# A linear-attention and expert block: x2 goes over DRAM to be turned on VectorE, with new orders on all engines

## What is computed

```python
h = layernorm(x) * (1 + ca) + sa
q, k = elu(h @ Wq.T + bq) + 1, elu(h @ Wk.T + bk) + 1;  v = h @ Wv.T + bv      # 16 heads of 32
KV = sum_s k v ;  Z = 1 / (q . sum_s k + 1e-6)
x1 = x + ga * ((q KV Z) @ Wo.T + bo)
x2 = layernorm(x1)
V  = (x2 * (1 + cb) + sb) @ fWv.T + fbv                                         # 512 wide
r, c = V @ Wg.T + bg, norms of 8 probes of 8 of V                               # 8 experts
w  = softmax over the top 2 of  ln(r) + sigmoid(alpha) * ln(c)
out = x1 + gb * (V + sum_e w_e * (silu(V @ W1_e.T + b1_e) @ W2_e.T + b2_e))
```

## Time and profile before

| what | value |
|---|---|
| median of three runs | 1216.82 us |
| the profiled execution: its time, its span | 1216.84 us, 1215.1 us |
| TensorE, VectorE busy over the span | 1202.4 us (99%), 1001.0 us (82%) |
| GpSimd, ScalarE busy over the span | 609.1 us (50%), 545.0 us (45%) |
| DMA queues | 34.6% of 16 engines, 108 GB/s |
| granted TensorE clock | 9 or more tenths in all 40 slices |

### The profile page before, as it was taken

How to read it: one execution, slowest core, us unless ns; L and a number is a source line. 1 busy time by engine, 2 the same in 40 slices (tenths; PEclk the granted TensorE clock), 3 DMA queues, 4 the chain that set the end, 5 groups by cost and what they waited for, 6 DMA issues and landing times.

```text
span 1215.1 us, 18365 instructions
## 1 busy us (share of the span) xinstructions
PE 1202.4 (99%) x5680; PEld 987.7 (81%) x5680; DVE 1001.0 (82%) x2218; ACT 545.0 (45%) x1127; POOL 609.1 (50%) x458
## 2 busy tenths in 40 slices
PE   8999999999999999999999999999999999999998
PEld 5888878787877787887778888888888888888887
DVE  6988788988889888886788888888887888888775
ACT  4455454454454545454534343443434343443432
POOL 1443433333333443444556575766657576675741
PEclk9999999999999999999999999999999999999999
DMA  6565544444343343443231322313232231322201
GB/s 225 166 192 180 159 129 143 139 138 125 111 131 107 119 129 120 124 139 112 79 96 61 96 77 81 104 53 104 63 95 88 70 105 53 105 70 88 87 19 53
DMA packets 128515, 131.65 MB, mean 108 GB/s; under 512 B 12233, under 2 KB 82289, under 8 KB 128417
## 3 DMA queue, kind: packets, MB, share of 16 engines
q1 hardware_dynamic: 128416, 130.47, 34.6%
HBM read 80.62 MB, written 49.81 MB: 107 GB/s over the span
## 4 chain that ended last, share of the span: by engine, by line
PE 85%; DVE 5%; issue 4%; ACT 3%; DMA 1%; POOL 1%; SPq 0%; POOLq 0%; DVEq 0%; ACTq 0%
PE ps L1637 26%; PE ps L1638 26%; PE ps L1644 26%; PE ps L1853 3%; PE ps L1845 1%; DMA wm_in<-in_L_wmod_dram 1%; PE ps L1745 1%; DVE zk L1306 1%; DMA q_in<-q_scratch 1%; ACT exp_k L859 1%; ACT exp_q L830 1%; DVE qf L1282 1%; ACT exp_q L832 1%; POOL cn L725 1%; ACT exp_k L861 0%
## 5 line engine op out<-in xcount | busy, mean ns | idle before, releaser
L696 POOL TENSOR_TENSOR xn_lo<-xn,xn_hi 128x512 fp32r<-128x512 f32 x64 | 85.9, 1342 | 279.6 <-ACT xn_hi L821 279.6
L725 POOL TENSOR_TENSOR cn<-c,half 128x16 f32<-128x16 f32 x32 | 104.1, 3254 | 189.8 <-DVE c L1405 189.8
L830 ACT ACTIVATE exp_q<-qf 128x512 f32<-128x512 f32 x64 | 40.5, 632 | 150.5 <-DVE qf L1282 150.3
L1637 PE MATMUL ps<-wk_hi,xT_hi 128*128 128x512 f32 x256 | 101.8, 398 | 2.3 <-ACT xT_hi L815 2.3
L1637 PE MATMUL ps<-g_hi,qT_hi 128*128 128x512 f32 x256 | 103.2, 403 | 0.1
L1637 PE MATMUL ps<-v_hi,xT_hi 128*128 128x512 f32 x256 | 103.0, 402 | 0.0
L1637 PE MATMUL ps<-k_hi,xn_hi 128*128 128x512 f32 x256 | 102.7, 401 | 0.0
L1637 PE MATMUL ps<-wq_hi,xT_hi 128*128 128x512 f32 x256 | 102.5, 400 | 0.1
L1638 PE MATMUL ps<-wq_lo,xT_hi 128*128 128x512 f32 x256 | 101.4, 396 | 0.0
L1638 PE MATMUL ps<-wk_lo,xT_hi 128*128 128x512 f32 x256 | 101.3, 396 | 0.0
L1638 PE MATMUL ps<-k_lo,xn_hi 128*128 128x512 f32 x256 | 100.6, 393 | 0.0
(11 more groups left out here) (250 smaller groups left out, 3333.8 us busy)
## 6 DMA issues: line engine op xcount, KB each, us to landing
xin<-_attn_hidden_states_dram SPq DMA_DIRECT2D x64, 256.0 KB, 3.1
q_scratch<-qf SPq DMA_DIRECT2D x64, 256.0 KB, 3.3
xin<-_attn_hidden_states_dram SPq DMA_DIRECT2D x32, 512.0 KB, 4.2
q_in<-q_scratch SPq DMA_DIRECT2D x128, 128.0 KB, 2.9
out_dram<-qf SPq DMA_DIRECT2D x64, 256.0 KB, 2.0
xn_scratch<-xn SPq DMA_DIRECT2D x62, 256.0 KB, 2.0
xq<-xn_scratch SPq DMA_DIRECT2D x248, 64.0 KB, 2.5
wm_in<-in_L_wmod_dram SPq DMA_DIRECT2D x4, 1024.0 KB, 6.1
```

The source lines that it names most:

```text
L696: nc.gpsimd.tensor_tensor(moved(xn_lo[:, 1 - s, :], i + 1), kept(xn[:, 1 - s, :], i + 1), moved(f32(xn_hi[:, 1 - s, :]), i + 1), ALU.subtr ...
L725: nc.gpsimd.tensor_tensor(cn[:].rearrange("p h e -> p (h e)"), c2[:].rearrange("p h e -> p (h e)"), half[:], ALU.pow).then_inc(cn_done, 1)
L830: nc.scalar.activation(exp_q[:, s, :], zq[:, s, :], ACT.Relu, scale=-1.0).then_inc(rq_done, 1)
L1637: nc.tensor.matmul(dst, ah, bh, start=start and n == 0, stop=False)
```

## The change

For the pairs 3 to 30, x2 isn't turned by TensorE any more. ScalarE writes the normalised tile in another order of its 32-column blocks, SyncE stores it to a scratch in DRAM (`x2_store`), loads it back in four pieces with the blocks regrouped over the partitions (`x2_load`, into the new buffer `x2q`), and VectorE turns the 32x32 blocks into the PSUM bank (`turned_x2`), where ScalarE and VectorE split it as before. The two `turn_hidden` of a pair become one, with five transposes in a row, and the high and low parts of both halves are taken by one instruction each (`aT_high(j)`, `aT_low(j)`, 512 wide). `qT_low` moves to GpSimd for the first pairs too. The orders of all five engines are new: on TensorE both `out_product` come first in a step and `fused_product` behind them; on VectorE `scores` and `weights` of a pair stand together at the end of the step; on GpSimd the power of the probes stands behind `queries_low`, and `q_times_ks` of pair j + 3 follows directly on `biased_x` of pair j + 1.

Left out of the diff are declarations, the waits that go with the new counts and the code ahead of the first full step. The functions `step_b` of GpSimd, ScalarE, VectorE and TensorE stand with their new text alone, in this order; the old ones stand above.

```diff
+            sp.wait_ge(qz_done, 3)
+            q_load(4)
+            sp.wait_ge(xb_done, 3)
+            bx_load(3)
+            def x2_store(j, h):
+                sp.wait_ge(x2_done, 2 * j + h + 1)
+                sp.dma_start(x2_dram[rows(2 * j + h), :], xn[:, h, :]).then_inc(x2_out[h], 16)
+            def x2_load(j, h):
+                sp.wait_ge(x2_out[h], 16 * (j - 2))
+                wait_count(sp, x2T_turned, 2 * (j - 4) + h + 1)
+                for i in range(KB):
+                    sp.dma_start(x2q[DH * i:DH * (i + 1), h, :].rearrange("p (g f) -> p g f", f=P),
+                                 x2_dram[rows(2 * j + h), i * P:(i + 1) * P].rearrange("(g t) f -> t g f", t=DH)).then_inc(x2_back[h], 16)
+            def result_store(j, h):
+                sp.wait_ge(fin_done, 2 * j + h + 1)
+                sp.dma_start(ot[rows(2 * j + h), :], out_t[:, h, :]).then_inc(stored[h], 16)
-                if live(j + 2, J):
-                    sp.wait_ge(qz_done, j + 1)
-                    q_load(j + 2)
-                if live(j + 1, J):
+                if live(j + 3, J):
+                    sp.wait_ge(qz_done, j + 2)
+                    q_load(j + 3)
+                if j > 2 and live(j + 1, J):
-                for h in range(2):
-                    if live(j - 2, J):
-                        sp.wait_ge(fin_done, 2 * (j - 2) + h + 1)
-                        sp.dma_start(ot[rows((j - 2) * 2 + h), :], out_t[:, h, :]).then_inc(stored[h], 16)
+                if live(j, J) and not by_pe(j):
+                    for h in range(2):
+                        x2_store(j, h)
+                        x2_load(j, h)
+                        result_store(j - 2, h)
+                else:
+                    for h in range(2):
+                        if live(j - 2, J):
+                            result_store(j - 2, h)
...
+            queries_low(3)
             def step_b(j):
                 if live(j + 2, J):
                     q_times_ks(j + 2)
+                if live(j + 1, J):
+                    queries_low(j + 1)
                 if live(j, J):
                     row_scale(j)
+                probe_norms(j - 1)
+                router_scale(j - 1)
                 if live(j + 1, J):
                     biased_x(j + 1)
+            sweep_pairs(step_b, 3, J)
...
-                act.wait_ge(x2T_psum, t + 1)
+                if j < FIRST_TURNED:
+                    act.wait_ge(x2T_psum, t + 1)
+                elif by_pe(j):
+                    act.wait_ge(x2T_psum, 2 * FIRST_TURNED + h + 1)
+                else:
+                    act.wait_ge(x2T_turned, 2 * (j - FIRST_TURNED) + h + 1)
...
+            def aT_high(j):
+                act.wait_ge(aT_psum, j + 1)
+                wait_count(act, y_psum, 2 * j)
+                nc.scalar.copy(wT_hi[:], bank_qaT[:, 2 * P:3 * P])
+                nc.scalar.copy(aT_hi[:], two_aT).then_inc(aTh_done, 1)
...
-                wait_count(act, x2T_psum, t - 1)
+                if j <= FIRST_TURNED:
+                    wait_count(act, x2T_psum, t - 1)
+                else:
+                    act.wait_ge(x2_out[h], 16 * (j - FIRST_TURNED))
...
-                nc.scalar.activation(xn[:, h, :], x1_of(j, h), ACT.Identity, bias=shift[:, h:h + 1],
+                dst, src = (xn[:, h, :], x1_of(j, h)) if by_pe(j) else (quarters(xn[:, h, :]), natural(x1_of(j, h)))
+                nc.scalar.activation(dst, src, ACT.Identity, bias=shift[:, h:h + 1],
...
             def step_b(j):
+                if j > 3 and live(j + 1, J):
+                    qT_high(j + 1, 0)
                 if live(j, J):
                     deviations(j, 0)
+                if j > 3:
+                    x2T_high(j - 1, 1)
+                if j == 3:
+                    qT_high(4, 0)
+                if live(j + 1, J):
+                    qT_high(j + 1, 1)
                 if live(j, J):
                     deviations(j, 1)
                     variances_eps(j)
+                aT_high(j - 2)
+                if live(j + 2, J):
+                    den_plus_eps(j + 2)
+                functions(j - 1)
+                if live(j, J):
                     normalised(j, 0)
                     normalised(j, 1)
                 if live(j, J):
                     x2T_high(j, 0)
+                exponentials(j - 1)
+            sweep_pairs(step_b, 3, J)
+            aT_high(J - 1)
         @block.vector
...
+            def turned_x2(j, h):
+                dve.wait_ge(x2_back[h], 64 * (j - 2))
+                dve.wait_ge(x2Tl_done, 2 * j + h)
+                dve.wait_ge(aTl_done, j - 1)
+                nc.vector.transpose(bank_x2T.rearrange("p (j g t) -> p g j t", j=KB, g=KB),
+                                    x2q[:, h, :].rearrange("p (g j f) -> p g j f", g=KB, j=KB)).then_inc(x2T_turned, 1)
...
+            def aT_low(j):
+                dve.wait_ge(aTh_done, j + 1)
+                nc.vector.tensor_tensor(aT_lo[:], two_aT, f32(aT_hi[:]), ALU.subtract).then_inc(aTl_done, 1)
...
             def step_b(j):
                 if live(j, J):
                     residual(j, 0)
+                if j == 3:
+                    scaled_q(4)
+                    turned_q(4)
+                elif not by_pe(j - 1):
+                    turned_x2(j - 1, 1)
                 if live(j, J):
                     residual(j, 1)
+                if j > 3:
+                    x2T_low(j - 1, 1)
                 if live(j + 2, J):
                     denominators(j + 2)
+                biased(j - 1, 0)
+                aT_low(j - 2)
+                if live(j + 2, J):
+                    inverses(j + 2)
+                biased(j - 1, 1)
+                probes(j - 1)
+                gated(j - 1)
+                finished(j - 2, 0)
+                if live(j + 2, J):
+                    scaled_q(j + 2)
+                finished(j - 2, 1)
+                variances(j - 1)
+                if live(j + 2, J):
+                    turned_q(j + 2)
+                if live(j, J) and not by_pe(j):
+                    turned_x2(j, 0)
                 if live(j, J):
                     x2T_low(j, 0)
+                scores(j - 1)
+                weights(j - 1)
+            sweep_pairs(step_b, 3, J)
+            aT_low(J - 1)
             finished(J - 1, 0)
             finished(J - 1, 1)
...
-            def turn_hidden(j, h):
-                t = 2 * j + h
+            def turn_hidden(j):
-                if bank_h(j, h) is bank_qaT:
-                    wait_count(pe, aTl_done, t)
-                else:
-                    pe.wait_ge(x2Tl_done, t + 1)
-                if h == 0:
-                    nc.tensor.transpose(bank_qaT[:, 2 * P:3 * P], ws[:], ident[:])
-                turn(bank_h(j, h), aw[:, h, :], 2).then_inc(aT_psum, 1)
+                wait_count(pe, aTl_done, j)
+                pe.wait_ge(x2Tl_done, min(2 * j + 4, T))
+                nc.tensor.transpose(bank_qaT[:, 2 * P:3 * P], ws[:], ident[:])
+                turn(bank_qaT, aw[:, 0, :], 2)
+                turn(bank_x2T, aw[:, 1, :], 2).then_inc(aT_psum, 1)
+                wait_count(pe, aTl_done, j - 1)
...
             turn_x2(1, 1)
             def step_b(j):
                 if live(j, J):
                     out_product(j, 0)
                     out_product(j, 1)
+                fused_product(j - 1, 0)
+                turn_hidden(j - 2)
+                fused_product(j - 1, 1)
+                expert_product(j - 2, 0)
+                expert_product(j - 2, 1)
+                value_product(j - 1, 0)
+                if live(j, J) and by_pe(j):
                     turn_x2(j, 0)
+                value_product(j - 1, 1)
+                if live(j, J) and by_pe(j):
                     turn_x2(j, 1)
             sweep_pairs(step_b, 2, J - 1)
             fused_product(J - 1, 0)
             fused_product(J - 1, 1)
+            turn_hidden(J - 2)
             value_product(J - 1, 0)
             expert_product(J - 2, 0)
+            expert_product(J - 2, 1)
             value_product(J - 1, 1)
+            turn_hidden(J - 1)
             expert_product(J - 1, 0)
             expert_product(J - 1, 1)
...
```

More of the change, by code:

```diff
@@ L118, in build @@
     ot = out.rearrange("a (t p) d -> (a t p) d", p=P)
+    x2_dram = nc.dram_tensor("x2_scratch", [T * P, D], F32, kind="Internal").ap()
     xn_dram = nc.dram_tensor("xn_scratch", [T * P, D], F32, kind="Internal").ap()
@@ L228, in build @@
         qks = sb("qks", [P, 2, D], F32, late)
+        x2q = sb("x2q", [P, 2, D], F32, late)
         den = sb("den", [P, 2, HEADS], F32, late)
@@ L398, in build @@
         x2T_psum = sem("x2T_psum")
+        x2T_turned = sem("x2T_turned")
+        x2_out = [sem("x2_out0"), sem("x2_out1")]
+        x2_back = [sem("x2_back0"), sem("x2_back1")]
         x2Th_done = sem("x2Th_done")
@@ L432, in bank_v, with by_pe @@
             return bank_o(h) if j == J - 1 else bank_y(h)
-        def bank_h(j, h):
-            return bank_x2T if (j, h) == (J - 1, 1) else bank_qaT
```

(90 more changed lines are left out.)

36 lines of the change are left out of this document (removed).

## The result

| | before | after |
|---|---|---|
| median | 1216.8 us (4 runs) | 1277.32 us (4 runs, 1277.08 to 1277.58) |
| ratio | | 1.0497 [1.0484, 1.0509] |
| profiled execution: its span | 1215.1 us | 1275.4 us |
| from `residual(3,0)` to `residual(31,0)` | 643.03 to 1181.00 | 641.43 to 1233.79 |

The account below looks back on a forecast made before the run. TensorE was taken to bound the kernel before at 19.26 us a pair, and VectorE's twice-held chain the changed one at 20.95. 1216.8 + 47.3 for 28 steps + 1 for step 3 = 1265 us, range 1225 to 1288.

Parts of the forecast that it names:

- the two products named: GpSimd's q times ks, forecast to hold the first multiply of scores, and queries_low, forecast to hold the gating in weights.
- 16.9 less 15.85: First hold: scores could start at 15.85 us into a step, but its first multiply waits for q times ks until about 16.9.
- the table: Forecast timetable of one step from residual(j,0), each engine in its new order: 18.9 us without holds, 20.95 with both.
- the second hold: In weights on VectorE: the gating aw, due at 19.2 us, waits for GpSimd's queries_low until about 20.1.
- the case given 21.1: In weights: if the small L1473 is caught by queries_low as well, weights end at 21.1 us instead of 20.8.
- TensorE's own pace: TensorE's work a pair falls from 19.26 to 18.3 us; the rival that it stays the bound, 1191 us, had 0.05.
- The power doesn't hold the gate: GpSimd's power leaves VectorE's gate at its plain 0.69 us; the rival that it holds it, 1340 us, had 0.02.
- The sum: The whole kernel's forecast time: 1216.8 us before, plus 47.3 and 1, gives 1265 us.
- 47.3 + 1: 28 steps longer by 1.69 us each, plus about half of the 2.3 us of scaled_q(4) and turned_q(4) in step 3.
- a rival of its own: TensorE's clock falls to 1.2 GHz as it waits in each pair: +2 us a step, about 1320 us; chance 0.04.
- the old order's length stands: At the kernel's end no q is left to be multiplied, so the end was forecast to last as long as before.
- The inner 1255 to 1277: Whole-kernel time with both holds, allowing a third of a microsecond a step either way; chance 0.62.

Follow-up runs that it names:

- e3: The changed kernel with all x2 turned by TensorE and nothing over DRAM, the new orders alone: 1268.59 us, 1.0425 of the kernel before.
- e1: The changed kernel with one more GpSimd wait, so q times ks starts only behind the gating aw: 1213.08 us, 0.9966 of the kernel before.
- e6: The changed kernel with q times ks behind aw, and scores moved ahead of x2T_low(j,0) on VectorE: 1203.21 us, 0.9886 of the kernel before.
- e8: The changed kernel with VectorE's and ScalarE's last step in the order of the kernel before: 1271.89 us, 1.0452 of the kernel before.
- e2: The changed kernel with only queries_low behind aw on GpSimd, q times ks still early: 1245.77 us, 1.0236 of the kernel before.
- e7: The changed kernel with 8 small matmuls of constants ahead of turn_hidden's waits on TensorE: 1274.62 us, 1.0474 of the kernel before.

## Why the prediction was right, step by step

- **Direction and mechanism**: right. A step is set by VectorE's chain, held twice, beside the two products named. Forecast 20.95 us, measured 20.94 to 20.96 in undisturbed steps. L1505 was held by 1.7 where 16.9 less 15.85 gives 1.05: in the step shown x2 came back 0.7 us earlier than by the table (`turned_x2(j,0)` at 13.15 and not 13.8; the last load landed after 2.0 us and not 2.5), so the hold was entered earlier and ended at the same instant. That error costs nothing, as the product's end decides.
- **Where the second hold fell**: half right. It caught the small L1534 (0.93), the case given 21.1; the rest of the table ran 0.15 early and made up for it. The prediction had the gating `aw` held as well, with 1.3 to 1.6 us as a sign of being right; it took its plain 0.68, as `queries_low` was over by then. So the agreement to a hundredth is luck: a step would have come out at 21.1 with this hold, had the rest of the table been exact.
- **The orders, not DRAM**: e3 shows it, 20.85 a step without any x2 over DRAM. The prediction had both in one chain; it had said that the holds cost 2.05 of 20.95, and e1 measures 2.55 in undisturbed steps (20.95 less 18.4).
- **TensorE's own pace** of 18.3: 18.4 in e6.
- **TensorE's wait** of 2 to 3 us, ended by `x2T_low`: 2.36. VectorE's before `turned_x2(j,0)`, put at 1.5: 0.9 in the step shown, up to 2.5.
- **The power doesn't hold the gate**: right, 0.69 in every step. The Trainium skill ("SBUF — State Buffer", Who interferes with whom) gives the shared ports to whichever instruction issues first, for the whole of it. For the products the trace agrees, as L1505 ends 0.05 us behind q times ks; for the power of 2.90 us it doesn't.
- **The sum**: 12 us low. Its terms by the trace: the entry came 1.6 us earlier (641.43 against 643.03). From `residual(3,0)` to `residual(31,0)` it grew by 54.4 where 47.3 + 1 were forecast. Seven stretches at half the clock are 7 by 1.2 = 8.4 of that; this was a rival of its own, priced at 2 us in every step, and it came in one step of four and at 1.2. The last two steps have less work (19.47 and 18.39), which gives 4.0 back. The 28 steps of the kernel before take 19.21 on average and not 19.26, which adds 1.3. And the end took 7.5 us more, where "the old order's length stands" was the step that failed: the last pair's routing now stands behind waits for pair 30, and e8 returns 4.5 us of it.
- **The range** of 1225 to 1288 held. The inner 1255 to 1277 rested on steps without dips and an end of the old length, and was missed by 0.3 us.

## What to carry to other kernels

When the busiest engine is relieved, lay out one step of the next one as a chain with all its waits, GpSimd's products included: VectorE had 15.0 us of work by the prediction's sum, in a step of 18.3, and needed 20.95. An order of GpSimd that is "as early as the data allow" isn't free: a product of 2.4 us put beside a run of small VectorE instructions with two SBUF inputs costs what is left of it (1.7 us here), while the same product behind them costs nothing (e1). Such a hold doesn't show among the waits of a profile, only as a long duration of a small instruction. Where two engines have the same pace, some slack in the one with DMA waits is worth more than its size, since it takes up late landings: covering 0.65 us of VectorE's waiting gave 10 us over 28 steps (e6).

## What the runs showed of the hardware that was not expected

- A cast with a single SBUF input (L1541, 128x32) was held too: 1.25 us beside `queries_low` in e3, where it takes 0.18 elsewhere. So having two inputs isn't needed.
- A power and the gate (L1420 before) met one way round only. In the kernel before the gate starts 0.16 us ahead of the power in 30 of 32 pairs, and the power lasts 3.28 us; in the last two the power starts 0.16 ahead, and both take their plain 2.90 and 0.69. Why the power is lengthened but doesn't hold isn't shown.
- TensorE's granted clock fell to 1.2 GHz now and then where it had waited 2.0 to 2.4 us once a step: 3.4 us each time, in seven of 28 steps. With waits of 1.45 us (e2) and 1.34 us (e3) it didn't in steps 4 to 30, nor with 8 small matmuls in the wait (e7).
